# Adding the residual of a dense tile on TensorE and copying the result out on ScalarE, in place of VectorE's addition

## The reference

```
x1  = x + ssm(ctx, layernorm(x))      # a state-space layer, 16 states per channel
out = x1 + ffn(layernorm(x1))         # a dense layer plus a routed low-rank part
ffn(h) = h @ W_base.T + b_base + sum over the 2 best of 8 experts of gate_e * 2 * (h @ A_e.T) @ B_e.T
```

## Time and profile before

| What | us |
|---|---|
| median of 3 executions | 2297.03 |
| lowest and highest of them | 2294.46, 2306.67 |
| the profiled execution, its own time | 2301.22 |
| its span, first to last instruction | 2299.4 |

### The profile page before, as it was taken

The page is one execution under the profiler, slowest core; times in us unless marked ns, Lnnn a source line. Parts: engine busy times, 40 slices in busy tenths (PEclk is TensorE's granted clock), DMA queues, the critical chain, the costliest instruction groups (busy, mean ns, idle before and its releaser), DMA issues.

```text
span 2299.4 us, 23586 instructions
## 1 busy us (share of the span) xinstructions
PE 1871.5 (81%) x7968; PEld 1125.1 (49%) x7968; DVE 1768.0 (77%) x1412; ACT 1267.3 (55%) x1707; POOL 1804.4 (78%) x812
## 2 busy tenths in 40 slices
PE   8677777766778888888988888888888788778888
PEld 3244444444455455555554555555555455454444
DVE  3388888878898888877888898888989999992101
ACT  3455555545566656546566665556666666643222
POOL 0288888889988888889988888899999999993010
PEclk9777777769779998889889998899999999999998
DMA  4655455575655555676655555676766655652121
GB/s 140 228 220 185 157 190 176 189 255 198 237 184 180 194 199 181 208 270 217 227 174 192 199 194 194 203 255 213 250 205 205 210 202 203 209 191 71 62 71 46
DMA packets 157977, 435.85 MB, mean 190 GB/s; under 512 B 14528, under 2 KB 47552, under 8 KB 157728
## 3 DMA queue, kind: packets, MB, share of 16 engines
q1 hardware_dynamic: 157856, 434.34, 55.4%
HBM read 383.43 MB, written 50.86 MB: 189 GB/s over the span
## 4 chain that ended last, share of the span: by engine, by line
PE 37%; DVE 26%; issue 13%; POOL 13%; ACT 6%; DMA 5%; SPq 0%; DVEq 0%; POOLq 0%; ACTq 0%
DVE state L993 17%; POOL prod L1121 8%; PE y_ps L460 8%; PE bank_b L412 8%; PE bank_a L514 7%; DVE row L980 5%; DVE conv L972 3%; PE row L454 3%; POOL drive_rows L1114 2%; PE bank_b L514 2%; PE row L536 2%; DMA decay<-yy_d 2%; PE bank_a L525 2%; POOL x L1129 1%; DMA conv<-u_d 1%
## 5 line engine op out<-in xcount | busy, mean ns | idle before, releaser
L1121 POOL TENSOR_TENSOR prod<-state,c_rows 128x1024 f32<-128x1024 f32 x512 | 1200.5, 2357 | 198.9 <-DVE state L993 162.1
L993 DVE TENSOR_TENSOR_SCAN state<-decay,row 128x1024 f32<-128x1024 f32 x320 | 730.6, 2283 | 5.2
L460 PE MATMUL y_ps<-ident,prod 128*128 128x128 f32 x4096 | 628.0, 304 | 125.9 <-POOL prod L1121 120.5
L460 PEld LDWEIGHTS y_ps<-ident,prod 128*128 128x128 f32 x4096 | 542.1, 157 | 338.9 <-POOL prod L1121 220.6
L980 DVE TENSOR_TENSOR row<-du,row 128x1024 f32<-128x1024 f32 x320 | 388.2, 1213 | 103.3 <-PE row L454 72.4
L1114 POOL TENSOR_TENSOR drive_rows<-du,b_rows 128x1024 f32<-128x1024 f32 x192 | 453.8, 2364 | 0.1
L993 DVE TENSOR_TENSOR_SCAN state<-row,drive_rows 128x1024 f32<-128x1024 f32 x192 | 435.5, 2268 | 21.2 <-POOL drive_rows L1114 15.0
L514 PE MATMUL bank_a<-w_o,xnT 128*128 128x512 f32 x816 | 395.4, 601 | 1.3 <-DVE x L1044 1.3
L454 PE MATMUL row<-parts,sel 96*128 96x512 bf16 x640 | 221.5, 432 | 205.1 <-DVE state L993 194.7
L750 ACT ACTIVATE decay<-delta,a 128x1024 f32<-128x1024 f32 x320 | 359.8, 1135 | 0.1
L750 ACT ACTIVATE row<-delta,a 128x1024 f32<-128x1024 f32 x192 | 214.2, 1116 | 243.8 <-DVE state L993 242.9
(11 more groups left out here) (103 smaller groups left out, 1730.8 us busy)
## 6 DMA issues: line engine op xcount, KB each, us to landing
c_rows<-bc_d SPq DMA_DIRECT2D x512, 512.0 KB, 4.1
xrow<-in_x SPq DMA_DIRECT2D x32, 512.0 KB, 7.1
u_d<-conv SPq DMA_DIRECT2D x32, 512.0 KB, 5.4
skip<-u_d SPq DMA_DIRECT2D x32, 512.0 KB, 6.0
yy_d<-yy SPq DMA_DIRECT2D x32, 512.0 KB, 6.3
x<-in_x SPq DMA_DIRECT2D x32, 512.0 KB, 6.8
b_rows<-bc_d SPq DMA_DIRECT2D x24, 512.0 KB, 5.4
conv<-u_d SPq DMA_DIRECT2D x48, 256.0 KB, 5.5
```

Of the source, the lines that this page charges most:

```text
L460: last = nc.tensor.matmul(y_ps[:, i * P:(i + 1) * P], source[:, i * P:(i + 1) * P], ident[:, :], start=(first and i % (H // P) == 0), stop ...
L993: nc.vector.tensor_tensor_scan(state[:, q % STATES, :], factor, term, 0.0, ALU.mult, ALU.add).then_inc(scan_done, 1)
L1121: nc.gpsimd.tensor_tensor(prod[:, q % PRODS, :], state[:, q % STATES, :], c_rows[:, q % RING, :], ALU.mult).then_inc(prod_ready, 1)
```

## The change

Each half of a dense tile's product begins with one more matmul: the identity matrix against 512 columns of x1, which puts x1 into the bank, and the eight products and the ninth add to it. ACT then copies the bank to where DVE had written the sum (`take_result`, an activation of kind Copy) and signals `res_ready`. DVE's `add_residual` is gone. In a block, ACT's copies stand in sections 0 and 13, as DVE's additions did; in the tail both copies of tile j stand after `exp_gap(j+1)`, at the end of ACT's list for tile j. On DVE the tail is now `choose(j)` alone for each tile.

```diff
@@ product (PE)
+                if 0 in ks:
+                    nc.tensor.matmul(at.sums[h][:, :], ident[:, :], x1[:, j % 2, half(h)], start=True, stop=False)
                 for k in ks:
-                    nc.tensor.matmul(at.sums[h][:, :], at.xnT[:, k, :], w_o[:, k, half(h)], start=(k == 0), stop=False)
+                    nc.tensor.matmul(at.sums[h][:, :], at.xnT[:, k, :], w_o[:, k, half(h)], start=False, stop=False)
@@ new on ACT
+            def take_result(j, h, at):
+                act.wait_ge(o_ready, 2 * j + h + 1)
+                if j < FIRST_TAIL:
+                    to = x1[:, j % 2, half(h)]
+                else:
+                    after(act, res_out[h], 16 * j)
+                    to = res_tail[:, h, 0:H]
+                nc.scalar.activation(to, at.sums[h][:, :], ACT.Copy).then_inc(res_ready, 1)
@@ ACT, section(E, m)
+                if m == 0 and j >= 1:
+                    take_result(j - 1, 1, beside)
                 if m == 0:
                     scale_skip(E)
...
+                if dense and m == 13:
+                    take_result(j, 0, beside)
                 if j >= -1:
                     if m == 13:
                         row_sum(j + 1)
@@ ACT, tail
+            take_result(FIRST_TAIL - 1, 1, beside)
...
                     take_routing(j + 1, then)
                     exp_gap(j + 1)
+                for h in range(2):
+                    take_result(j, h, alone_at(j))
@@ DVE
-            def add_residual(j, h, at):
...
-                nc.vector.tensor_tensor(to, x1[:, j % 2, half(h)], at.sums[h][:, :], ALU.add).then_inc(res_ready, 1)
...
-                if m == 0 and j >= 1:
-                    add_residual(j - 1, 1, beside)
...
-                if dense and m == 13:
-                    add_residual(j, 0, beside)
...
-            choose(FIRST_TAIL)
             for j in range(FIRST_TAIL, NT):
-                add_residual(j, 0, alone_at(j))
-                if j + 1 < NT:
-                    choose(j + 1)
-                add_residual(j, 1, alone_at(j))
+                choose(j)
```

More of the change, by code:

```diff
@@ L1035, in gates @@
                                                ALU.mult, ALU.mult).then_inc(g_ready, 1)
-            def add_residual(j, h, at):
-                dve.wait_ge(o_ready, 2 * j + h + 1)
-                if j < FIRST_TAIL:
-                    to = x1[:, j % 2, half(h)]
-                else:
-                    after(dve, res_out[h], 16 * j)
-                    to = res_tail[:, h, 0:H]
-                nc.vector.tensor_tensor(to, x1[:, j % 2, half(h)], at.sums[h][:, :], ALU.add).then_inc(res_ready, 1)
             dve.wait_ge(ch_in, 16)
@@ L1080, in _ @@
                     section(E, m)
-            add_residual(FIRST_TAIL - 1, 1, beside)
             gated_y(NBLK - 1)
```

## The result

| | before | after |
|---|---|---|
| median of 4 executions each, us | 2301.85 | 2328.06 |
| ratio, 95% interval | | 1.0121 (1.0074 to 1.0169) |
| profiled execution, own time / span, us | 2301.22 / 2299.4 | 2328.6 / 2326.8 |
| PE matmul busy, us | 1871.5 | 1909.6 |
| DVE busy, us | 1768.0 | 1734.1 |

26 to 28 us slower, outside the range of 2262 to 2314.

The account below looks back on a forecast made before the run. POOL was taken as full in late blocks and waiting for DVE's scans in middle ones. Terms -9 + 0 + 0.86 + 1.72 - 0.8 + 1 - 5 = -11.2 us from 2301.2 gave 2290, median 2286; range 2262 to 2314.

Parts of the forecast that it names:

- Late blocks, 0: Blocks 24 to 31: POOL stays full, so nothing changes; 0 us, between 0 and +8.
- Start and end of the tail, +0.86 and +1.72: PE's identity matmuls add 0.86 us at the end of block 31 and 1.72 us in the last tile.
- Ring: -0.8, +1: Repeating tail tiles: ACT's shorter copy of half 1 saves 0.8 us; stores nearer the loads cost 1 us.
- the clock's -5: Tail: a shorter PE pause may keep the clock up, recovering a third of 15 us; -5, between 0 and -15.
- Middle blocks, -9: Blocks 9 to 23: DVE's relief gains 0.9 us in nine blocks (-8), three others -1 us together.
- Behind `experts` PE has no longer 1.05 us of idle time: Middle-block border: PE reaches the next row just in time; the chain to the projection gains 0 to 1.6 us, taken as 0.9.
- Blocks 14, 22 and 23 have no such halves: 0: Three middle blocks without the two or three halves of the others were forecast to change by 0 us.
- PE's half 1 so starts 1.1 us later: Section 13: ACT's copy behind two decays delays PE's half 1; with the identity matmul, everything behind is 2.0 us later.
- the slower rival: Section 13: PE's late half 1 outweighs DVE's relief beyond 2.4 us; +16 and +3 us, 2316 us, chance 0.20.
- the first rival: Nothing passes: section 4's identity matmul eats DVE's gain, POOL's long stretch hides the rest; +3 us, median 2300, chance 0.20.
- the forecast's 0.48: Chance given to the forecast, own range 2276 to 2296 us, half of it beyond 0.5%.
- 0.28 was counted as faster: The forecast's share in the 0.40 chance of a faster kernel, which was 0.12 + 0.28.

## Why the prediction was wrong

*Late blocks, 0.* Right: 391.5 against 391.7 us, although the cover was thin as said (POOL once waits 0.64 and once 0.35 us for `y_ps` at a border; the blocks absorb it).

*Start and end of the tail, +0.86 and +1.72.* The end is right: 37.4 to 37.6 us in the runs with these matmuls in the last tile ahead of its products, 35.8 to 35.9 without. The start, +1.0 in the profile, is not shown: the stretch took 71.2 to 73.3 us with the matmuls (the run with the slow addition left out) and 71.7 to 72.6 without.

*Ring: -0.8, +1 and the clock's -5.* -0.4 in the profile after. PE's pause shrank to 1.8 to 2.7 us in seven of the eight tiles (0.33 in the first), as forecast (1.5 to 2.5). The clock did not follow: behind these seven pauses it still fell (mean 0.57 to 0.73 from the ninth matmul to the routing, 6.1 to 7.6 us), and only behind the 0.33 us it stayed up (4.64 us). The eight tiles took 51.7 us there before and 49.4 after, so that 2 of the 15 us came back, not 5. The same tail code took 164.0 to 169.7 us in eleven profiles, 167.0 on average, and that of the kernel before 167.9, 170.1 and 173.0 in three. A gain of some 3 us is likely, and one profile could not show it.

*Middle blocks, -9.* This is the step that failed: +30.3. The forecast followed DVE correctly as far as it went. For the border of a typical block it said that the drive of state 15 comes 0.8 us late, the drive of state 0 1.0 us late, and then the scan of state 0 1.4 us and the drive of state 2 1.15 us early; measured in the seven blocks: 0.9 and 1.2 late, 1.1 and 0.9 early. What failed is what it made of that, in four parts:

1. "Behind `experts` PE has no longer 1.05 us of idle time; it comes to the next row just in time" was true, and I booked it as a gain that lasts to the projection, between 0 and 1.6 us. A loss was not in that range. PE and DVE arrive early in section 3, PE pauses 1.8 to 1.9 us for POOL there instead of in section 1, and the half clock falls on the routing and what follows. The 0.9 us of gain at state 2 is a delay of 2.6 to 2.8 us at state 7: 18.4 us in seven blocks, of which filling the pause gave back 13. The price of the half clock is seen by itself in the run with the matmul last, 3.4 us between blocks 16 and 19.
2. The two borders of sequences and the first dense block were missed: "Blocks 14, 22 and 23 have no such halves: 0" looked only at the projection. PE does other products there and was busy 22.00 of 22.20 us: the drives of states 15 and 2 come 1.7 to 1.9 us late at the two borders. Blocks 9, 15 and 23 hold 8.7 us.
3. "PE's half 1 so starts 1.1 us later, and with its identity matmul everything behind it on PE is 2.0 us later" was worked out at full clock. In blocks 12 and 21 PE came out of its wait for the copy at half clock, and the drive of state 15 came 3.3 and 2.7 us late, beyond the 2.4 us that the slower rival named as its deciding point; the blocks behind, 13 and 22, were 1.0 and 2.1 us longer.
4. The 0.9 us of DVE's relief per block is nothing by itself (middle 968.1 with the relief alone). DVE's two places lie in the 45 us in which POOL never waits. I had that against me in the first rival and overrode it by following one chain. It is not lost for good: in block 16 of the run with the matmul last, at full clock, the scan of state 7 starts 1.4 us earlier than before.

The slower rival had the place, half 1's late start behind ACT's decays, and the copy's position did cost 18 us. Its mechanism, a delay at scan 0 beyond DVE's relief, held in two blocks only; elsewhere that scan was at most 0.1 us late. Its 1 us per middle block measured 2, its 0.5 us per late block 0. That it pointed the right way is in part luck. In the chances, half of the forecast's 0.48 would be 0.24, where 0.28 was counted as faster.

The Trainium skill ("Perfetto Trace Analysis", "Identifying the Most-Contended Engine") judges TensorE's headroom by MFU (the share of its peak arithmetic) and the share of weight loads. I took the 49% of weight loads as room in which the identity matmuls would be free. In this case that share misled: they cost 12 us of middle blocks even when placed best.

What stays open: why a pause of one length is followed by half clock in one block and by full clock in another, how the 30 us divide between half clock and PE's lateness (with the pause back in section 1 and DVE loaded again, nothing was gained), and why the second wait of POOL stays 1 us longer with the pause filled. The excess of the five middle blocks outside both groups, 3.2 us, was not looked into.

## What to carry to other kernels

When work moves to an engine that feeds others, the position of the release in the new engine's list can cost more than the work: here two decays ahead of one copy per block cost 18 us, the matmuls 12. An engine that gets ahead of its consumer pauses further down its list. A pause that a change removes is not a gain until the trace says where it goes; if that engine's clock falls behind pauses, follow the half clock to the work that it will cover. The most striking border need not be the one that costs: block 12 into 13 is one of two of its kind. Relief of an engine counts only where its consumer waits within reach of the relieved place; a kernel with only that part of the change shows its worth in one run.

## What was unexpected of the hardware

- **More work made it faster.** 9 us more of transposes on PE, in pauses of 1.9 us, took some 19 us off the median. In the changed kernel the clock was at half level behind each of the seven pauses of 1.8 to 1.9 us; with 0.6 us left of them in six of the blocks it was not in any.
- **The same pause with two outcomes.** 1.9 us of pause in section 3 were followed by half clock in six blocks and by full clock in three of one execution (the matmul last, above). In the kernel before with the repeated matmul, pauses of 0.20 and 0.42 us in block 10 were followed by half clock, 0.20 and 0.44 in block 11 by full clock; the blocks took 64.2 and 61.9 us:

```profile
734.23 1.80 PE L462 MATMUL y_ps<-ident,prod 128*128 128x128 f32 x8 [0.42 <-POOL prod L1123]
735.96 2.07 PE L422 MATMUL bank_b<-xd,w_bdt 32*128 32x512 f32 x2
...
798.49 1.09 PE L462 MATMUL y_ps<-ident,prod 128*128 128x128 f32 x8 [0.44 <-POOL prod L1123]
799.51 1.12 PE L422 MATMUL bank_b<-xd,w_bdt 32*128 32x512 f32 x2
```

- **DVE's addition by where its operands lie.** 128x512 float32 took 2668 ns with both operands in SBUF beside POOL's products and 688 ns with one of them in PSUM; POOL's late blocks grew from 391.5 to 426.7 us with the former, to 397.7 with the latter. The residual's addition had one operand in PSUM.
